# Routing of the first four steps, and the scatters of the first three, moved from the feed-forward stage into the stage ahead of it

## What is computed

```python
def _moe(x, ...):                                   # x: the normalised stream, T x 256
    shared = silu(x @ ws_gate) * (x @ ws_up) @ ws_down
    scores = sigmoid(x @ gate_w.T)                  # 16 experts
    topk_w, topk_idx = top_k(scores, 2)
    topk_w = topk_w / (topk_w.sum(-1) + 1e-20) * 2.5
    eo = einsum(silu(x @ w_gate[e]) * (x @ w_up[e]), w_down[e])   # 256 -> 128 -> 256
    return sum over the two chosen experts of topk_w * eo + shared
```

## Time and profile before

| | us |
|---|---|
| three executions | 2522.54, 2528.37, 2533.62 |
| the profiled execution: its own time | 2514.77 |
| its span in the trace | 2513.1 |
| merge stage, first instruction to the next stage's first | 1096.8 to 1153.98 |
| first feed-forward, front up to the first tile load | 1153.98 to 1270.62 |
| output stage | 2132.0 to 2216.83 |
| second feed-forward, front up to the first tile load | 2216.83 to 2336.30 |

### The profile page before, as it was taken

How to read it: one execution, slowest core, us unless ns; L and a number is a source line. 1 busy time by engine, 2 the same in 40 slices (tenths; PEclk the granted TensorE clock), 3 DMA queues, 4 the chain that set the end, 5 groups by cost and what they waited for, 6 DMA issues and landing times. The chain is left out here.

```text
span 2513.1 us, 107266 instructions
## 1 busy us (share of the span) xinstructions
PE 2097.4 (83%) x43952; PEld 1629.5 (65%) x43952; DVE 1817.8 (72%) x4507; ACT 1553.0 (62%) x3824; POOL 1521.3 (61%) x3168
## 2 busy tenths in 40 slices
PE   8889999999999999988679442899999997885793
PEld 5557777777777777766368442677777775663682
DVE  6689999999989999946446561677777775764466
ACT  5578888888888888824323220677666773663231
POOL 3357778878777787785645366345454454355462
PEclk9989999999999999999889755999999998988896
DMA  6921112111121121133357543111111111743456
GB/s 215 278 55 45 43 46 50 48 43 43 50 72 43 46 52 45 31 128 144 117 185 232 165 161 118 52 53 53 50 53 49 45 37 38 241 152 110 132 157 232
DMA packets 188836, 245.65 MB, mean 98 GB/s; under 512 B 41672, under 2 KB 144981, under 8 KB 187456
## 3 DMA queue, kind: packets, MB, share of 16 engines
q1 hardware_dynamic: 161824, 182.08, 24.2%
q0 software_dynamic: 19872, 50.41, 5.8%
q10 hardware_dynamic: 6656, 6.31, 0.8%
HBM read 136.08 MB, written 106.50 MB: 97 GB/s over the span
## 5 line engine op out<-in xcount | busy, mean ns | idle before, releaser
L671 ACT ACTIVATE at_E<-at_S,at_mn 128x1024 f32<-128x1024 f32 (+7 forms) x704 | 592.7, 846 | 60.4 <-DVE at_mn L740 49.9
L740 DVE TENSOR_REDUCE at_mn<-at_S 128x1 f32<-128x1024 f32 (+3 forms) x448 | 484.6, 1098 | 3.5 <-PE at_S L850 2.8
L891 PE MATMUL at_pcs<-at_E,at_c 128*32 128x256 f32 (+1 forms) x4864 | 409.3, 338 | 2.4 <-issue 2.3
L850 PE MATMUL at_S<-am_sk,am_sq 96*32 96x512 bf16 (+3 forms) x4608 | 392.1, 348 | 8.6 <-issue 2.4
L608 POOL TENSOR_TENSOR at_kvo<-am_kh,am_vh 128x256 f32<-128x256 f32 x512 | 304.7, 629 | 0.1
L1362 POOL DMA_INDIRECT expert_out<-m_ysb,m_dst x158 | 155.4, 984 | 127.7 <-DVE m_dst L1544 114.0
L891 PEld LDWEIGHTS at_pcs<-at_E,at_c 128*32 128x32 f32 x4864 | 219.2, 109 | 20.5 <-issue 5.6
L593 POOL TENSOR_TENSOR at_half<-at_half 128x128 f32<-128x128 f32 (+4 forms) x640 | 185.3, 290 | 50.1
L661 ACT ACTIVATE at_Tt<-at_S,at_mn 128x192 f32<-128x192 f32 x512 | 174.0, 428 | 63.6 <-DVE at_mn L728 63.2
L850 PEld LDWEIGHTS at_S<-am_sk,am_sq 96*32 96x32 bf16 x4608 | 160.5, 97 | 72.0 <-ACT at_E L671 29.8
L891 PE MATMUL at_pcs<-at_Tt,at_c 128*32 128x128 f32 x1024 | 177.5, 274 | 0.6 <-issue 0.4
(11 more groups left out here) (393 smaller groups left out, 5636.9 us busy)
## 6 DMA issues: line engine op xcount, KB each, us to landing
m_xg<-expert_rows SPq DMA_DIRECT2D x158, 129.0 KB
am_sq<-q_parts SPq DMA_DIRECT2D x192, 64.0 KB, 2.3
am_sk<-k_parts SPq DMA_DIRECT2D x192, 64.0 KB, 2.3
memory_rows<-m_blank SPq DMA_DIRECT2D x16, 516.0 KB
gl_hx<-memory_rows SPq DMA_DIRECT2D x32, 258.0 KB, 3.4
m_wgu<-in_f_wgu SPq DMA_DIRECT2D x2, 4096.0 KB, 14.0
rt_yin<-expert_out SPq DMA_DIRECT2D x7, 1024.0 KB, 9.7
fn_yin<-expert_out SPq DMA_DIRECT2D x7, 1024.0 KB, 8.6
```

Of the source, the lines that this page charges most:

```text
L671: ins = nc.scalar.activation(E[:, at:at + w], S[v % NS_B][:, i * CW:i * CW + w], ACT.Exp, bias=mn[:, q, s, 1 + j:2 + j], scale=-1.0, accum ...
L740: nc.vector.tensor_reduce(mn[:, q, :, :].rearrange("p s k -> p (s k)")[:, at[0]:at[0] + 1], S[v % NS_B][:, 0:w], AX.X, ALU.min).then_inc(s ...
L850: ins = nc.tensor.matmul(S[v % NS_B][x, at:at + cw], sq[:, u, t * P + x.start:t * P + x.stop], sk[:, u, c0 + c:c0 + c + cw], start=True, s ...
L891: ins = nc.tensor.matmul(pcs[j * R:(j + 1) * R, cols[0]:cols[1]].rearrange("p (b c) -> p b c", c=P), lhsT, rhs, start=(n, j) not in touche ...
```

## The change

A class `Routing` now holds the routing's tiles, semaphores and code; one object is made ahead of each feed-forward and handed to both stages. The merge and the output stage now do the routing of steps 0 to 3 (`ROUTED` = 4), normalise the rows of steps 0 to 4 (`AHEAD` = 5; before: 4 in the merge, 1 in the output stage) and send the scatters of steps 0 to 2 (`SENT` = 3). For that they gain, for each of four steps: 8 transposes of the normalised rows and their two copies (`turn_rows`, `turned`), the logits, the exponential, `pick` and `ranks` and `place`. The feed-forward's front still does the shared expert of all 8 steps, in the order `TURNS`, and routes steps 4 to 7. In the output stage the silu is halved and its PSUM buffer is 3 halves and not 4, to make room.

```diff
+GT = 4
+WIDE = GT * P
+STEPS = T // WIDE
+ROUTED, AHEAD, SENT = 4, 5, 3
...
+    def scatter(self, pool, n, a, z):
+        if a == 0:
+            pool.wait_ge(self.s_e2, n + 1)
+            pool.wait_ge(self.s_slot, n + 1)
+            if n:
+                pool.wait_ge(self.sent, n * GT * TOPK * 16)
+        for t in range(n * GT + a, n * GT + z):
+            for j in range(TOPK):
+                pool.indirect_dma_start(out=self.xs, out_offset=bass.IndirectOffsetOnAxis(ap=self.slot[:, t, j:j + 1], axis=0),
+                                        in_=self.hx[:, t, :], in_offset=None).then_inc(self.sent, 16)
...
-                if n >= 8 and n % 2 == 0 and (n - 8) // 2 < K:
-                    scale_of((n - 8) // 2)
+                if n == 3:
+                    rt.constants(pool)
+                if n >= 6 and n % 2 == 0:
+                    scale_of(n // 2 - 3)
+                if n >= 10 and (n - 10) // 2 < SENT:
+                    rt.scatter(pool, (n - 10) // 2, n % 2 * GT // 2, (n % 2 + 1) * GT // 2)
...
+                if n >= 8 and n % 2 == 0 and (n - 8) // 2 < ROUTED:
+                    rt.place(dve, (n - 8) // 2, p_c)
                 add_rows(n)
-                if n >= 2 and n % 2 == 0 and n // 2 - 1 < K:
+                if n >= 2 and n % 2 == 0 and n // 2 - 1 < AHEAD:
                     stats_of(n // 2 - 1)
+                if n >= 7 and n % 2 and (n - 7) // 2 < ROUTED:
+                    rt.pick(dve, (n - 7) // 2)
...
+                k = (n - 8) // 2
+                if n >= 8 and n % 2 == 0 and k < ROUTED:
+                    rt.ranks(pe, k, p_c)
                 if n + 1 < NS:
                     turn(n + 1)
+                k = (n - 5) // 2
+                if n >= 5 and n % 2 and k < ROUTED:
+                    turn_rows(k, 0)
                 project(n)
...
-        SETS = ((1, 2), (2, 4), (4, NS)) if K == 1 else ((4, 6), (6, NS))
+        SETS = ((5, 6), (6, NS))
+        TURNS = (4, 5, 6, 0, 7, 1, 2, 3)
...
-            for n in range(NS):
-                if n == 1:
+            for n in range(SENT, NS):
+                if n == SENT + 1:
                     scale_of(LAST)
...
+                if n == 1:
+                    rt.constants(pool)
+                if n >= 3:
+                    scale_of(n - 3)
+                if n == NS - 1:
+                    rt.scatter(pool, 0, 0, G)
+            for n in range(1, SENT):
+                rt.scatter(pool, n, 0, G)
...
+                if n >= 4 and n - 4 < ROUTED:
+                    rt.pick(dve, n - 4)
                 if n:
                     residual(n - 1)
-            dve.wait_ge(s_z, 2)
...
+                if n >= 4 and n - 4 < ROUTED:
+                    rt.place(dve, n - 4, p_c)
+                if n and n - 1 < AHEAD:
+                    stats_of(n - 1)
             residual(NS - 1)
```

`pick`, `place`, `ranks`, `logits` and `exps` hold the instructions that the front's loop held, in the same order and shapes. The new ones around them in the merge stage (the output stage has the like, with steps shifted):

```diff
+            def turned(k, c):
+                act.wait_ge(s_R, KC * k + c + 1)
+                if k and c == 0:
+                    act.wait_ge(rt.s_log, k)
+                nc.scalar.copy(rT[:, c, :], p_R[:, :]).then_inc(s_rT, 1)
...
+            def turn_rows(k, c):
+                pe.wait_ge(s_hn, (k + 1) * GT)
+                if k or c:
+                    pe.wait_ge(s_rT, KC * k + c)
+                for t in range(GT):
+                    ins = nc.tensor.transpose(p_R[:, t * P:(t + 1) * P], hx[:, k * GT + t, c * P:(c + 1) * P], ident[:, :])
+                ins.then_inc(s_R, 1)
```

More of the change, by code:

```diff
@@ L991, in phase_merge @@
+def phase_merge(nc, x, q_full, Y, kvc, q0, x0, wc_s, kv_dram, own, state, keep, hx, rt, gate):
     with ExitStack() as ctx:
@@ L1381, in silu @@
                 nc.scalar.activation(act_g[:, :], p_g[:, :], ACT.Silu).then_inc(s_act, 1)
[L1383 to L1384 removed]
+            for i, n in enumerate(TURNS):
                 for k in range(KC):
[L1386 to L1398 removed]
+                    act.wait_ge(s_T, i * KC + k + 1)
+                    if k == 0 and i >= 2:
+                        act.wait_ge(s_gu, i - 1)
+                    nc.scalar.copy(hT[:, i % 2, k, :], p_T[k][:, :]).then_inc(s_hT, 1)
+                if i + 1 < NS and TURNS[i + 1] >= K:
+                    front(TURNS[i + 1])
+                if i:
+                    silu(i - 1)
+                if n >= ROUTED:
+                    rt.exps(act, n, p_log)
             silu(NS - 1)
@@ L1500, in _ @@
+            for i, n in enumerate(TURNS):
+                if i:
+                    hidden(i - 1)
+                if n >= ROUTED:
+                    rt.pick(dve, n)
+                    rt.place(dve, n, p_rank)
+                if i == 0:
                     for later in range(*SETS[LAST]):
@@ L2819, in gates @@
             def gates(n):
-                act.wait_ge(s_g, n + 1)
                 if n >= 2:
                     act.wait_ge(s_gated, n - 1)
-                nc.scalar.activation(silu[:, n % 2, :], p_g[:, n % 2, :], ACT.Silu).then_inc(s_silu, 1)
+                for half in range(2):
+                    act.wait_ge(s_g, 2 * n + half + 1)
+                    nc.scalar.activation(silu[:, n % 2, half * 2 * D:(half + 1) * 2 * D], p_g[:, (2 * n + half) % 3, :],
+                                         ACT.Silu).then_inc(s_silu, 1)
             def squares(n):
@@ L2836, in _, with front, turned @@
                 squares(n)
+            def front(k):
+                act.wait_ge(s_rstd, 4 * (k + 1))
+                for a in range(k * G, (k + 1) * G):
+                    nc.scalar.activation(hx[:, a, 0:D], acc[:, a, :], ACT.Identity, bias=nbias[:, a:a + 1],
+                                         scale=rstd[:, a:a + 1]).then_inc(s_hn, 1)
+            def turned(k, c):
+                act.wait_ge(s_R, KC * k + c + 1)
+                if k and c == 0:
+                    act.wait_ge(rt.s_log, k)
+                nc.scalar.copy(rT[:, c, :], p_T[:, c, :]).then_inc(s_rT, 1)
             for n in range(NS):
+                if n >= 3 and n - 3 < ROUTED:
+                    front(n - 3)
                 for k in range(KC):
@@ L2844, in _ @@
                     gates(n + 2)
+                if n >= 3 and n - 3 < ROUTED:
+                    turned(n - 3, 0)
+                    turned(n - 3, 1)
+                if n + 2 < NS:
                     squares(n + 2)
-            act.wait_ge(s_rstd, 4)
-            for a in range(G):
-                nc.scalar.activation(hx[:, a, 0:D], acc[:, a, :], ACT.Identity, bias=nbias[:, a:a + 1],
-                                     scale=rstd[:, a:a + 1]).then_inc(s_hn, 1)
-            act.wait_ge(s_hn, G)
+                if n >= 3 and n - 3 < ROUTED:
+                    rt.exps(act, n - 3, p_l)
+            front(ROUTED)
+            act.wait_ge(s_hn, NR)
         @block.vector
@@ L2929, in turn @@
                     pe.wait_ge(s_yT, n * KC)
+                if n >= 4:
+                    pe.wait_ge(s_rT, min(n - 3, ROUTED) * KC)
                 for k in range(KC):
@@ L2953, in _ @@
                     gates(n + 2)
-                project(n)
+                if n >= 3 and n - 3 < ROUTED:
+                    turn_rows(n - 3, 0)
+                    turn_rows(n - 3, 1)
+                if n >= 4 and n - 4 < ROUTED:
+                    rt.ranks(pe, n - 4, p_c)
+                project(n)
+                if n >= 3 and n - 3 < ROUTED:
+                    if n == 3:
+                        pe.wait_ge(rt.gate_in, 16)
+                    pe.wait_ge(s_rT, KC * (n - 2))
+                    rt.logits(pe, n - 3, rT, p_l)
 def build(nc, a, ctx):
```

516 lines of the change are left out of this document (276 added, 240 removed).

## The result

The changed kernel takes 2568.48 us (median of 4 runs, 2562.61 to 2570.86), the kernel before in the same comparison 2530.47: ratio 1.014, 95% interval 1.011 to 1.0171. It is slower by 38 us, inside the range and 13.5 us above the forecast of 2555.

The account below looks back on a forecast made before the run. Merge: GpSimd and TensorE near their limits; first front: GpSimd's scatters; output stage: VectorE works 6.84 of 8.11 a step. Terms +47, -27, +35.6 and -28.5 sum to +27, on the median 2528.4 giving 2555 us; range 2530 to 2574.

Parts of the forecast that it names:

- The first wait of 8 us: Merge: GpSimd waits about 8 us ahead of its first scatter, until VectorE has written `slot` of step 0.
- the 6.8 of a front's step without routing: Feed-forward fronts: a TensorE step that only does the shared expert takes 6.8 us, one that routes 8.87.
- the pads as the end of the fronts: Fronts: the first tile load follows ScalarE's pad writes, not the last scatter, at 88 to 91 us.
- The merge, +47: Merge stage: 37.4 us more ahead of the last state, plus a longer tail; middle of 41 and 53.
- the waits for `slot` 1 and 2: Merge: GpSimd's waits for the slots of steps 1 and 2, taken as 1.3 us each.
- GpSimd is near its limit, and 20 scatters go in: Merge: 20 scatters of 1.26 us stand ahead of the last state on GpSimd, 25.2 us, and waits come with them.
- 24 scatters leave each front ...; in the stages ahead the same scatters stand in full on the path: Whole change: fronts lose 37 us of scatters but give back only 27 to 28; earlier stages pay in full, with waits.
- The clock: Merge: TensorE's granted clock may fall; +41 us at full clock, +53 at 1.2 GHz, middle taken; the three cases together 0.77.
- First front, -27: First feed-forward front: TensorE's and ScalarE's chain sets the end instead of scatters; 27 us shorter, bounds -25 and -29.
- Output stage, +35.6: Output stage: 24 scatters stand behind GpSimd's last power and the next stage starts 0.5 later; 35.6 us longer.
- Second front, -28.5: Second feed-forward front: the same steps as in the first, 119.5 us to about 91.
- little is lost in the merge waits: Rival, merge: VectorE keeps up, slot and statistics waits vanish; sum +14, or +11 with the tail unchanged, 2539; chance 0.12.

Follow-up runs that it names:

- warm_fill2: The changed kernel with 8 extra, useless matmuls of 256 columns in each TensorE merge step from the tenth on; ratio to the kernel before 1.0113.
- pads: The changed kernel with 12 of the 16 blocks of empty rows written by SyncE and 4 by ScalarE (before 8 and 8); ratio to the kernel before 1.0138.
- out_spread: The changed kernel with 12 of the output stage's 24 scatters issued earlier, behind the scales of its sixth and seventh iteration; ratio to the kernel before 1.0083.
- late_ranks: The changed kernel with all its scatters, TensorE's ranks in the merge stage moved behind project(n); ratio to the kernel before 1.014.
- two_groups: The kernel before, with two semaphores in turn, so a scatter group waits for the landing of the group before the last; ratio to the kernel before 0.9873.

## Why the prediction was right or wrong

- **The direction** was right and the size, +27, was 11 short of the +38 measured. The first wait of 8 us (8.32), the last power (83.5 us into the stage; 83.9), the 1.26 between scatters, the 6.8 of a front's step without routing and the pads as the end of the fronts stand in the trace as forecast.
- **The merge, +47, came as 51.6, by a sum that was wrong in its parts.** Ahead of the last state it grew by 43.6 (forecast 37.4): the waits for `slot` 1 and 2 were 3.5 each and not 1.3, which is 4.5 of the 6. The tail grew by 8.0 (9.9 to 17.9): 2.9 of it stand there at full clock too (warm_fill2; forecast 3.2 to 3.5), 5.1 are the clock. The step that failed is "GpSimd is near its limit, and 20 scatters go in" as the whole cause: it put the wait on `pick` only where GpSimd waits for `slot`, and left out that TensorE waits for the same `pick` at its `ranks`, that its logits hold up ScalarE's normalised rows, and that its transposes and `project` stand behind all of these. It named what is queued behind GpSimd's wait and not what is queued behind TensorE's. Without any scatter the stage is 29.3 longer. The two causes overlap, so the sum came out near; that was luck.
- **"24 scatters leave each front ...; in the stages ahead the same scatters stand in full on the path"**, the prediction's reading of the loss, is wrong: the early scatters cost 41.2 and save 39.0. The loss is the routing, 36 of the 38. In the output stage the prediction had the routing alone at 15 (VectorE's end); without early scatters the stage is 21.1 longer.
- **The clock**: it fell, 0.71 in the stretch. I took the middle of 41 and 53 for it, 6 us. In the tail it cost 5.1 in this profile and 1.5 in pads' with the same code; the slot waits, TensorE's part of which I had let double, gave nothing back: at clock 1.00 the stage up to the end of the last state was 1.6 longer, not shorter, though the extra matmuls count in that.
- **First front, -27**: -22.9 in this profile, and -26 to -29 in out_spread, late_ranks and warm_fill2, whose code there is the same. The mechanism was right. The first silu came 21.2 us into the stage (1225.08) and not at 19. From the first silu to the last it took 61.4 us and not 53.8: three of the seven steps fell to 6.8 as forecast, the other four took 8.4 to 12.3, where the forecast had three of 8.87 and a fourth of 6.8. The halts described above lie among them; in out_spread, without halts, the four took 7.5 to 9.6 and all seven 56.1. Behind the last silu it was shorter than forecast: 0.9, 7.65 for the pads and 2.6 to the load, 11.1 for 16.7.
- **Output stage, +35.6**: 40.1. The power and the scatters were right to 1 us; the barrier came 3.4 behind the last scatter, not 0.5. I had named that (2.4 if the barrier waits for the landing) and not taken it; the 0.5 stood in no row, the kernel before has 1.8 between VectorE's last row and the next stage.
- **Second front, -28.5**: -30.4.
- **Rivals**: the one in which "little is lost in the merge waits" did not come. What spoke for it, VectorE busy for only 20.6 of 32 us, was no help: the order in the loop counted, not the load. Scatters held GpSimd for 1.26 to 1.27 (1.3 to 1.5 for the first of four in the merge).
- The absolute time was forecast 13.5 us low: 11 from the sum, the rest from the medians (2528 and 2530).

## What to carry to other kernels

Work that is moved into a stage with two engines near balance can cost by the loop that it closes, not by its load: before adding a step that goes from TensorE to VectorE and back, write down for each engine what stands behind the wait, and follow the loop all the way round. Shortening one wait in it (3.1 to 0.8 at the ranks) left a pair of steps at 13.2 us for 13.4. When a move takes two things along, run it without one of them: here one cost 36 us and the other next to nothing, and the sum that blamed the wrong one still came out right. Before a gain of 3 us is put down to an edit, look at another run with the same code in that stage: pads had it in the merge stage without any edit there. And look first at the bound where it stands: one wait in the fronts of before, for the landing of the last group where the one before that does, was worth 31.5 us in a few lines.

## What the runs showed of the hardware

- Short VectorE instructions in `pick` take longer while GpSimd works on a state: `r_oh` 1.13 us at 1130.86, with GpSimd's product of 1129.38 to 1131.84 beside it, and 0.26 at 1157.51 with GpSimd idle; `pick` is about 1 us longer for it.

```profile
1130.86 1.13 DVE L1106 TENSOR_TENSOR r_oh<-r_iota_e,r_idx_f 128x128 f32<-128x128 f32 x1
...
1157.51 0.26 DVE L1106 TENSOR_TENSOR r_oh<-r_iota_e,r_idx_f 128x128 f32<-128x128 f32 x1
```

- The next stage came 3.36 us after the last indirect DMA had been issued in the changed kernel and 3.58 in out_spread; in the kernel before, with none there, it came 1.8 behind VectorE's last row. A group behind a landing waits 2.39 in the earlier trace rows. That the barrier waits for the landing is read from this and was not tried.
- With up to sixteen scatters under way instead of eight, GpSimd still issued one every 1.27 us (two_groups).
- The same kernel took 861.4 and 878.9 us over the same untouched stretch in two executions, and over all runs that stretch goes with the chip. Stages with the same code differ between profiles by up to 3 us in the merge stage (105.9 to 108.9, by the clock of its tail), 1.6 in the output stage (123.5 to 125.1) and 6 in the first front (87.4 to 93.8).
